# Query stage of a gated cross-attention block: a ring of row buffers, normalising on GpSimd, another order of projections

## What is computed

```
n1  = layernorm(x)                                   # no scale, no shift
q   = n1 @ wq + bq ; k = ctx @ wk + bk ; v = ctx @ wv + bv
x   = x + tanh(g_xattn) * (softmax(q k^T per head) v @ wo + bo)
x   = x + tanh(g_ffn)   * guided_self_attention(layernorm(x)) 
```

## Time and profile before

| | us |
|---|---|
| median of 3 runs | 2854.22 |
| lowest, highest | 2852.57, 2858.64 |
| profiled execution, its own time | 2863.41 |
| its span | 2861.5 |
| end of the query stage's last VectorE instruction | 126.1 |
| TensorE busy | 2642.9 (92% of the span) |
| VectorE, ScalarE, GpSimd busy | 1829.7, 1336.3, 372.3 |

### The profile page before, as it was taken

The page is one execution under the profiler, slowest core; times in us unless marked ns, Lnnn a source line. Parts: engine busy times, 40 slices in busy tenths (PEclk is TensorE's granted clock), DMA queues, the critical chain, the costliest instruction groups (busy, mean ns, idle before and its releaser), DMA issues. The chain is left out here.

```text
span 2861.5 us, 52305 instructions
## 1 busy us (share of the span) xinstructions
PE 2642.9 (92%) x17376; PEld 2361.2 (83%) x17376; DVE 1829.7 (64%) x2869; ACT 1336.3 (47%) x2994; POOL 372.3 (13%) x274
## 2 busy tenths in 40 slices
PE   5799999999999999999999999999949999579999
PEld 5689888988889888888988889888847777478887
DVE  6456676666766666666666766667646677436665
ACT  3235444554445554455544445444433444245654
POOL 0020110000110001110001100011013333100000
PEclk9899999999999999999999999999959999859999
DMA  5545444444544454444554445444339999788982
GB/s 174 176 127 122 120 107 119 118 113 120 119 112 111 120 122 117 105 119 111 121 121 117 119 103 124 119 120 102 92 111 177 187 199 201 152 168 191 194 186 76
DMA packets 367908, 380.02 MB, mean 133 GB/s; under 512 B 127950, under 2 KB 275310, under 8 KB 367726
## 3 DMA queue, kind: packets, MB, share of 16 engines
q1 hardware_dynamic: 317134, 358.18, 53.5%
q10 hardware_dynamic: 50592, 19.06, 3.4%
HBM read 162.57 MB, written 72.57 MB: 82 GB/s over the span
## 5 line engine op out<-in xcount | busy, mean ns | idle before, releaser
L649 DVE TENSOR_TENSOR c_parted<-c_prob,c_parted 128x600 fp32r<-128x600 f32 x512 | 400.9, 783 | 464.0 <-ACT c_prob L590 463.0
L586 ACT ACTIVATE c_parted<-c_pair 128x600 fp32r<-128x600 f32 x512 | 344.4, 673 | 375.5 <-PE c_pair L728 374.6
L635 DVE TENSOR_REDUCE c_peak<-c_pair 100x1 f32<-100x724 f32 x512 | 450.0, 905 | 76.8 <-PE c_pair L710 66.4
L532 POOL TENSOR_TENSOR c_ct_lo<-e_stage,c_ct_hi 128x722 fp32r<-128x722 f32 x128 | 224.7, 1757 | 1766.0 <-ACT c_ct_hi L561 1766.0
L742 PE MATMUL c_mix<-c_parted,c_v 128*66 128x200 f32 (+1 forms) x3072 | 379.0, 260 | 16.5 <-DVE c_q_stack L640 16.4
L728 PE MATMUL c_pair<-c_q_stack,c_k_stack 100*128 100x100 f32 (+1 forms) x3072 | 391.0, 264 | 0.0
L89 PE MATMUL c_work<-c_ct_hi,w_wk_hi 128*128 128x362 f32 (+1 forms) x1024 | 366.0, 357 | 20.1 <-POOL c_ct_lo L532 16.0
L728 PEld LDWEIGHTS c_pair<-c_q_stack,c_k_stack 100*128 100x128 f32 (+1 forms) x3072 | 375.2, 188 | 6.7
L568 ACT ACTIVATE c_v<-c_work 128x512 fp32r<-128x512 f32 x192 | 115.6, 602 | 527.2 <-PE c_work L91 527.2
L742 PEld LDWEIGHTS c_mix<-c_parted,c_v 128*66 128x66 f32 (+1 forms) x3072 | 327.2, 139 | 37.5 <-DVE c_q_stack L640 25.6
L89 PE MATMUL c_work<-w_wv_hi,c_ct_hi 128*128 128x512 f32 (+1 forms) x768 | 317.2, 413 | 34.4 <-issue 28.6
(11 more groups left out here) (162 smaller groups left out, 4155.6 us busy)
## 6 DMA issues: line engine op xcount, KB each, us to landing
c_k_stack<-c_k_hi SPq DMA_DIRECT2D x1024, 90.2 KB, 2.2
e_stage<-in_ctx SPq DMA_DIRECT2D x32, 1444.0 KB, 6.2
c_k_stack<-c_k_lo SPq DMA_DIRECT2D x512, 90.2 KB, 2.2
c_q_stack<-q_parts ACTq DMA_DIRECT2D x186, 100.0 KB, 3.2
mix_parts<-c_mixed SPq DMA_DIRECT2D x64, 200.0 KB, 3.2
r_parts<-mix_parts SPq DMA_DIRECT2D x50, 256.0 KB, 4.2
s_q_stack<-qk_parts SPq DMA_DIRECT2D x16, 800.0 KB
s_k_stack<-qk_parts SPq DMA_DIRECT2D x16, 800.0 KB
```

Of the source, the lines that this page charges most:

```text
L532: pool.tensor_tensor(ct_lo[odd][:, k, :], columns[:, k, :], ct_hi[odd][:, k, :], ALU.subtract).then_inc(ct_lo_done, 1)
L586: act.activation(parted[i % PR][:, :, 0, :].rearrange("p (a t) s -> p a t s", a=2), logits, ACT.Exp).then_inc(exp_hi_done, 1)
L635: dve.tensor_reduce(peak[:, i:i + 1], pair[i % 2][0:S, :, 0:HALF], AX.XY, ALU.max).then_inc(peak_done, 1)
L649: dve.tensor_tensor(p[:, :, 1, :], prob[i % 2][:], p[:, :, 0, :], ALU.subtract).then_inc(p_lo_done, 1)
```

## The change

1. `rows` becomes a ring of three buffers with a semaphore each; `stats`, `moments`, `std`, `rstd` and `normed` get two. SyncE issues rows 0, 1 and 2 without a wait; from then on the load of group g+3 waits until group g is normalised. `wq` is now loaded by ScalarE's queue.
2. Group 0 is still normalised by VectorE; groups 1 to 7 are normalised by GpSimd, with the same four instructions each.
3. TensorE's order is T(0), P(0), T(1), T(2), P(1), T(3), P(2), ..., T(7), P(6), P(7).
4. `wk` and `wv` are split after g = 1 and g = 3 (before: 0 and 5).
5. The first context is split in the query stage: ScalarE's `ct_hi` after g = 4, GpSimd's `ct_lo` between the normalising of groups 6 and 7. The tiles and semaphores of that buffer move to `CrossWeights`.
6. All loops of the stage are written out.

```diff
+ROW_BUFS = 3
+SPLIT_CROSS = (1, 3)
...
             def load(g):
-                sp.wait_ge(normed_ready, g)
-                sp.dma_start(rows[:], x_groups[g]).then_inc(rows_in, 16)
+                if g >= ROW_BUFS:
+                    sp.wait_ge(normed_ready, g - ROW_BUFS + 1)
+                sp.dma_start(rows[g % ROW_BUFS][:], x_groups[g]).then_inc(rows_in[g % ROW_BUFS], 16)
...
+        def normalise(engine, g):
+            at = g % 2
+            engine.wait_ge(rstd_ready, g + 1)
+            if g >= 2:
+                engine.wait_ge(turned_ready, (g - 1) * KT)
+            for r in range(GB):
+                last = engine.tensor_scalar(normed[at][:, r, :], rows[g % ROW_BUFS][:, r, :], moments[at][:, r, 0:1],
+                                            rstd[at][:, r:r + 1], ALU.subtract, ALU.mult)
+            last.then_inc(normed_ready, 1)
+
+        @block.gpsimd
+        def _(pool):
+            for g in range(1, GROUPS):
+                if g >= 2:
+                    pool.wait_ge(normed_ready, g)
+                normalise(pool, g)
+                if g == GROUPS - 2:
+                    pool.wait_ge(normed_ready, g + 1)
+                    for k in range(KT):
+                        pool.wait_ge(cross_w.ct_hi_done, k + 1)
+                        last = pool.tensor_tensor(cross_w.ct_lo[:, k, :], shared.columns[:, k, :], cross_w.ct_hi[:, k, :],
+                                                  ALU.subtract).then_inc(cross_w.ct_lo_done, 1)
...
             turn(0)
             pe.wait_ge(w_split, 2)
-            all_groups(pe, body)
+            project(0)
+            for g in range(1, GROUPS):
+
+                pe.wait_ge(xt_lo_ready, g * KT)
+                turn(g)
+                if g >= 2:
+                    project(g - 1)
+            project(GROUPS - 1)
...
-            split_columns(0, 0)
-            pool.wait_ge(ct_lo_done, KT)
...
-            for k in range(KT):
-                emit("split", k, 0, -1, 1)
```

More of the change, by code:

```diff
@@ L151, in stage_queries @@
         turned, product = bank[:4], bank[4:]
[L153 removed]
+        wq_in, bias_in, w_split = m.sem("wq_in"), m.sem("bias_in"), m.sem("w_split")
+        rows_in, rstd_ready = [m.sem(f"rows_in{i}") for i in range(ROW_BUFS)], m.sem("rstd_ready")
         eps_set, stats_seen = m.sem("eps_set"), m.sem("stats_seen")
@@ L214, in _, with statistics @@
             dve.memset(eps[:], EPS).then_inc(eps_set, 1)
-            STEPS = GB + GB + 1
-            def normalise(g, follows=True):
+            STEPS = GB + GB
+            def statistics(g):
+                at = g % 2
                 step = Tally(dve_step, g * STEPS)
-                dve.wait_ge(rows_in, g * 16 + 16)
+                dve.wait_ge(rows_in[g % ROW_BUFS], g // ROW_BUFS * 16 + 16)
                 for r in range(GB):
-                    step.done(dve.bn_stats(stats[:, r, :], rows[:, r, :]))
+                    step.done(dve.bn_stats(stats[at][:, r, :], rows[g % ROW_BUFS][:, r, :]))
@@ L231, in normalise, with split_rows @@
-                for r in range(GB):
-                    last = dve.tensor_scalar(normed[:, r, :], rows[:, r, :], moments[:, r, 0:1],
-                                             rstd[:, r:r + 1], ALU.subtract, ALU.mult)
-                last.then_inc(normed_ready, 1)
-            def split_rows(g, odd):
+                dve.reciprocal(rstd[at][:], std[at][:]).then_inc(rstd_ready, 1)
+            def split_rows(g):
                 for k in range(KT):
                     dve.wait_ge(xt_hi_ready, g * KT + k + 1)
-                    dve.tensor_tensor(xt_lo[odd][:, k, :], turned[k][:, 0:GS], xt_hi[odd][:, k, :],
+                    dve.tensor_tensor(xt_lo[g % 2][:, k, :], turned[k][:, 0:GS], xt_hi[g % 2][:, k, :],
@@ L255, in _ @@
-            normalise(0, False)
-            dve.wait_ge(loaded, 32)
-            dve.wait_ge(w_split, 1)
-            dve.tensor_tensor(w_lo[:], w_raw[:], w_hi[:], ALU.subtract).then_inc(w_split, 1)
-            split_rows(0, 0)
-            normalise(1)
+                    dve.scalar_tensor_tensor(q_lo[g % 2][:, k, :], product[k][:, 0:GS], bias[:, k:k + 1],
+                                             q_hi[g % 2][:, k, :], ALU.add, ALU.subtract).then_inc(q_lo_ready, 1)
             def split_cross(n):
@@ L265, in split_cross @@
                                   ).then_inc(cross_w.lo_done, 1)
-            all_groups(dve, body, split_cross)
+            statistics(0)
+            normalise(dve, 0)
+            dve.wait_ge(w_split, 1)
+            dve.tensor_tensor(w_lo[:], w_raw[:], w_hi[:], ALU.subtract).then_inc(w_split, 1)
+            split_rows(0)
+            statistics(1)
+            dve.wait_ge(bias_in, 16)
+            for g in range(GROUPS):
+                if g + 1 < GROUPS:
+                    split_rows(g + 1)
+                if g + 2 < GROUPS:
+                    statistics(g + 2)
+                split_queries(g)
+                if g in SPLIT_CROSS:
+                    split_cross(SPLIT_CROSS.index(g))
@@ L305, in split_cross, with split_columns @@
                 act.activation(cross_w.hi[n][:], cross_raw[n][:], ACT.Copy).then_inc(cross_w.hi_done, 1)
-            all_groups(act, body, split_cross)
+            def split_columns():
+                act.wait_ge(shared.columns_in, 16)
+                for k in range(KT):
+                    act.activation(cross_w.ct_hi[:, k, :], shared.columns[:, k, :], ACT.Copy
+                                   ).then_inc(cross_w.ct_hi_done, 1)
+            roots(0)
+            act.wait_ge(wq_in, 16)
+            act.activation(w_hi[:], w_raw[:], ACT.Copy).then_inc(w_split, 1)
+            split_rows(0)
+            roots(1)
+            act.wait_ge(bias_in, 16)
+            for g in range(GROUPS):
+                if g + 1 < GROUPS:
+                    split_rows(g + 1)
+                if g + 2 < GROUPS:
+                    roots(g + 2)
+                split_queries(g)
+                if g in SPLIT_CROSS:
+                    split_cross(SPLIT_CROSS.index(g))
+                if g == SPLIT_CROSS[1] + 1:
+                    split_columns()
         @block.tensor
```

113 lines of the change are left out of this document (40 added, 73 removed).

## The result

The kernel became slower: 2880.36 us median (2877.16 to 2886.52, 4 runs) against 2856.43 us (2852.57 to 2858.64, 4 runs), ratio 1.0081 with a 95% interval from 1.0057 to 1.0105. 2845.0 had been forecast, with a range from 2837 to 2857. The profiled execution has a span of 2879.4 us, 17.9 more than before.

What follows compares the result with a forecast made beforehand. TensorE's waits for `normed` in the query stage and its near idleness at the cross stage's start were taken as what matters; 2.6 + 6.6 = 9.2 us saved, 2854.2 - 9.2 = 2845.0 us, range 2837 to 2857.

Steps and rivals of the forecast that it cites:

- p: Time of one GpSimd normalising instruction in the query stage, four per group; taken as 0.8 us, between 0.48 and 1.13.
- part 3: Normalising on GpSimd: one input tile should cost less than two-input subtractions (1.13 to 1.37 us); 0.8 us per instruction taken.
- My range: Whole kernel: 2837 us (fast GpSimd, no late rows) to 2857 us (1.365 us per instruction, all key matmuls slow).
- fourth rival: Query stage: GpSimd's instruction costs still more, fetching two scalars per partition; at 1.76 us the kernel is 12.1 us slower; chance 0.08.
- the sum: Query stage added up group by group, waits and low clock included: end at some 123.5 us against 126.1, 2.6 us saved.
- Part 1: First loads: wq beside rows 0 shares the transfers, up to 3 us later rows; 1.3 us taken.
- Part 2: First projection moved ahead, starting at 20.5 instead of 30.34; most of the 11 us won given back at the second group.
- 4.8 + 4p: Gap in us between the transposes of groups 1 and 2: xt_lo, statistics, signals and four GpSimd instructions; 8.0 us taken.
- Part 4: Cost per later group: chain of 8.2 us hidden behind 8.8 us projection, except two 3.3 us waits at the weight splits.
- p = 0.94: GpSimd instruction time in us from which the per-group chain shows; each further 0.1 us costs 2.4 us.
- Part 5: Early split of the first context: the cross stage's first k_stack transfer comes 6.6 us earlier (5.7 to 7.5).
- the line at 2.5 us: TensorE's clock: a wait of 2.5 us or more may drop the clock and cost 1.9 us besides itself.

Runs made afterwards that it cites:

- forms run: Changed kernel with GpSimd running another form of its instruction in each group: 2.08 us two scalars and two operations, 1.49 one constant and one operation, 1.27 two-tile subtraction, 0.61 copy.
- ahead_on_gpsimd: Changed kernel with wq behind the rows, statistics one group ahead, wk/wv remainders on VectorE, next load before the store, GpSimd normalising groups 1 to 7: last q_lo 125.4 us.
- one_group_ahead: Changed kernel with VectorE normalising, wq behind the rows, statistics and normalising one group ahead, wk/wv remainders on GpSimd: ratio 0.9944 to the kernel before, last q_lo 114.7 us.
- first_order_of_before: Changed kernel with VectorE normalising, wq behind the rows, and TensorE's order of before (second group transposed before the first projection): last q_lo 114.2 us.
- vector_and_wq: Changed kernel with two edits, VectorE normalising all groups and wq loaded behind the rows of group 0: ratio 0.9975 to the kernel before, last q_lo 121.3 us.

## Why the prediction was wrong

**The step that failed is the size of p** (part 3). I bounded GpSimd's instruction by VectorE's 0.48 us and by GpSimd's instructions on two tiles (1.13 to 1.37 us; I called them subtractions, but lines 936 and 940 are additions), reasoned that an instruction with one tile as input must be cheaper than one with two, and took 0.8. It took 2.07. The rows that I called the upper bound were none, since they were of another form; the forms run shows that this form costs more than the subtraction, whatever its scalars. The rule of the Trainium skill that I quoted beside it ("GPSIMD Engine Reference", section Engine selection: one input is roughly line rate) fits the copy here (0.61 us for 512 columns, beside 0.54 of VectorE's `tensor_scalar`), and not this form (1.49 to 2.08 us). My range ended at p = 1.365, so it could not hold the result.

**The mechanism was the fourth rival's**, to which I gave 0.08: the same chain with a dearer instruction, slower from p = 1.49 on, and by 12.1 us at 1.76. With its own slope, 2.4 us for each 0.1, that gives 19.5 us at 2.07; 19.0 were measured at the first `k_stack` transfer. That they agree so closely is luck. With 2.07 the sum has T(2) at 45.0, and it began at 49.9 (2.3 us of later rows, 1.3 of wait before T(1), 0.7 of clock in P(0), 0.6 in the gap); the five groups from there to T(7) took 78.9 us instead of 84.2; and from T(7) to the last `q_lo` were 23.4 instead of 20.5, against an allowance of 3.0 us for the clock beside these terms. Its reason, the two scalars for each partition, was wrong: they cost 0.15 us. And its groups were not those that I had named: before T(4) and T(6) I expected the longest waits of the later groups, because of the weights' split (8.4 us each with 2.07); they were 3.4 and 3.9 us, like the others, since ScalarE and VectorE did the split while TensorE was late anyway.

**Part 1** was under-sized: 1.3 us were counted for `wq` beside the rows, 3.6 came (3.1 of them by the run with `wq` behind). The bound of 3 us was about right; the choice within it was not. The low clock was under-sized too: the sum has 5.9 us for it (1.0 in P(0), 1.9 at T(2), 3.0 at the two splits), and the matmuls took 98.05 us, about 15 more than eight groups of 10.36, since there were more and longer waits than the sum has. And the terms of the sum add up to 123.7, not 123.5.

**Part 2** was right in its core, that most of the head start is given back at the second group (gap 4.8 + 4p: 13.1 with p = 2.07, 13.7 measured), but not far enough: I did not put a price on keeping the order of before. The run with that order shows that this part of the change loses 7.0 us where VectorE normalises.

**Part 4.** The threshold p = 0.94 fits: with VectorE's 0.48 neither T(3) nor T(5) waited, and with GpSimd's 2.07 each did (4.5 us worked out for each; 4.36, 2.93 and 3.38 measured before T(3), T(5) and T(7)).

**Part 5** was right: 6.6 us forecast, 7.1 measured in the changed kernel, and a ratio of 0.9975 for it alone. That the rest of the program moves along was right as well (2711.7 and 2710.5 us), though this rest scatters by over 20 us between executions, so that the closeness of the two is chance.

**Contention.** I named the rule of the Trainium skill that a VectorE instruction with two SBUF inputs contends with GpSimd's reads ("SBUF — State Buffer", section Who interferes with whom) and saw no place for it. In the changed kernel that was right but for 0.3 us: `wk_lo` took 2.58 us beside GpSimd instead of 2.28. In the run `ahead_on_gpsimd` a normalising of GpSimd beside `wv_lo` took 1.4 us more. In two other experiments the two engines hindered one another in another instruction, the normalising, which reads one tile: by under 2 us in all with half on each engine, and by 7.3 us in `one_group_ahead`.

## What to carry over

Before work is moved to another engine, time that very form of instruction there; a row of another form is no bound, even if the form looks simpler. The chain from one group's last use of a buffer to the next group's first is what counts: the same 8.24 us on GpSimd cost 28 us more than VectorE's normalising in the chain, and 18 us more beside a projection, and VectorE's statistics, taken one group earlier in the program (with the weights' split and the loads moved to suit), made the stage 13.6 us shorter (121.3 to 107.7). An order that starts an engine earlier is worth only what the next wait leaves of it.

## What was not expected of the hardware

- GpSimd's `tensor_scalar` on 100 x 512 float32 takes 1.49 us with one operation, 2.08 with two and scalars per partition; a copy takes 0.61, a subtraction of two tiles 1.27.
- VectorE's `tensor_scalar` from SBUF to SBUF and GpSimd's `tensor_tensor` exclude one another for a whole instruction: 0.54 us became 4.78 beside a GpSimd instruction of 4.7. The Trainium skill ("SBUF — State Buffer", section Who interferes with whom) says of the port pair that VectorE and GpSimd share: "it's an exclusive lock". This trace agrees; the page has no time for this pair of instructions.
- Loads on ScalarE's and SyncE's queues shared the transfers about evenly: 1024 KB beside 800 KB delayed the latter by 3.1 to 3.6 us, and 800 KB are 3.1 us at the 262 GB/s of the earlier trace rows.
- Waits of 2.08 to 2.1 us before T(4) and T(6) were followed now by transposes at the full clock or nearly (1.56 us for T(6) in the run `first_order_of_before`, 1.88 for T(4) in `vector_and_wq`), now by the low one (2.90 us for T(4) in `first_order_of_before`). In the kernel before, a wait of 4.18 us before T(3) was followed by 2.21 us. So the line at 2.5 us that I had read from the earlier trace rows does not hold.
